# Mixture-of-experts stage on one core: expert outputs added into the output rows tile by tile

## The reference

```python
shared_out = (silu(x @ Wsg.T) * (x @ Wsu.T)) @ Wsd.T          # FS = 704
scores = softmax(x @ Wr.T)                                    # E = 8 experts
topk_scores, topk_idx = top_k(scores, 2)
w_full = sum(one_hot(topk_idx, E) * topk_scores[..., None])
out_e = (silu(x @ Wg[e].T) * (x @ Wu[e].T)) @ Wd[e].T         # F = 352, for every expert e
ffn = einsum('bsed,bse->bsd', out_e, w_full) + shared_out
out = x_before + gb * ffn                                     # gb: one row of 512 per batch
```

## Time and profile before

| what | us |
|---|---|
| median of 3 runs | 1969.69 (1968.26 to 1974.74) |
| profiled execution, span from first to last instruction | 1967.3 |
| busy in the span: TensorE | 1751.4 (89%) |
| VectorE, ScalarE, GpSimd | 1323.2 (67%), 716.7 (36%), 575.9 (29%) |
| GpSimd, the 64 gathers of the combination | 69.2 |

### The profile page before, as it was taken

One profiled execution on the slowest core, in us unless ns is written; L12 is line 12 of the kernel. 1 busy time (PEld: TensorE's weight loads), 2 busy tenths in 40 slices (PEclk: granted clock), 3 DMA queues, 4 the chain that ended last, 5 costly groups with the idle time before them and its releaser, 6 DMA issues.

```text
span 1967.3 us, 29963 instructions
## 1 busy us (share of the span) xinstructions
PE 1751.4 (89%) x9188; PEld 1523.2 (77%) x9188; DVE 1323.2 (67%) x2361; ACT 716.7 (36%) x1146; POOL 575.9 (29%) x691
## 2 busy tenths in 40 slices
PE   4599999997899999997999999999999999999800
PEld 0488888885777777776899999998999999999800
DVE  4899999965898898877432333326666666666566
ACT  2344444443433343333111111115554554554322
POOL 0343333323776676643144410000000000000076
PEclk8799999998998888887999999999999999999955
DMA  8333333327544334322455521105667767667387
GB/s 322 115 122 116 116 116 116 116 84 255 199 145 149 133 134 144 128 89 83 148 181 186 185 92 43 43 22 187 240 231 248 241 230 248 238 232 248 108 260 252
DMA packets 140152, 321.82 MB, mean 164 GB/s; under 512 B 20184, under 2 KB 20184, under 8 KB 134864
## 3 DMA queue, kind: packets, MB, share of 16 engines
q1 hardware_dynamic: 116080, 258.94, 39.4%
q0 software_dynamic: 12800, 41.95, 6.5%
q10 hardware_dynamic: 11232, 20.45, 2.7%
HBM read 213.23 MB, written 108.05 MB: 163 GB/s over the span
## 4 chain that ended last, share of the span: by engine, by line
PE 74%; DVE 14%; POOL 4%; issue 4%; DMA 3%; ACT 1%; SPq 0%; DVEq 0%; POOLq 0%; ACTq 0%
PE bank L424 17%; PE bank L426 17%; PE bank L425 17%; DVE mix L1280 5%; PE bank L1730 5%; PE bank L1728 5%; PE bank L1729 5%; PE bank L435 4%; POOL cb_y L863 3%; PE bank L1722 2%; DVE xh L1265 2%; DVE h_lo L1335 1%; PE bank L1678 1%; DMA stage<-in_w_k 1%; PE bank L1679 1%
## 5 line engine op out<-in xcount | busy, mean ns | idle before, releaser
L424 PE MATMUL bank<-gu_hi,ex_x_hi 128*128 128x352 f32 x1136 | 382.0, 336 | 0.8 <-DVE gu_lo L1362 0.8
L426 PE MATMUL bank<-gu_hi,ex_x_lo 128*128 128x352 f32 x1136 | 369.5, 325 | 0.0
L425 PE MATMUL bank<-gu_lo,ex_x_hi 128*128 128x352 f32 x1136 | 369.2, 325 | 0.0
L863 POOL DMA_INDIRECT cb_y<-expert_out_rows,slots x64 | 69.2, 1081 | 738.9 <-DMA expert_out_rows<-y_rows 719.7
L1478 DVE TENSOR_TENSOR hid<-bank,sg_t 128x352 f32<-128x352 f32 x142 | 74.5, 525 | 307.6 <-ACT sg_t L1015 307.6
L424 PEld LDWEIGHTS bank<-gu_hi,ex_x_hi 128*128 128x128 f32 x1136 | 216.1, 190 | 1.2 <-issue 1.2
L425 PEld LDWEIGHTS bank<-gu_lo,ex_x_hi 128*128 128x128 f32 x1136 | 216.1, 190 | 0.0
L426 PEld LDWEIGHTS bank<-gu_hi,ex_x_lo 128*128 128x128 f32 x1136 | 215.2, 189 | 0.0
L1015 ACT ACTIVATE sg_t<-bank 128x352 f32<-128x352 f32 x142 | 65.8, 464 | 396.6 <-PE bank L426 396.6
L1728 PE MATMUL bank<-dn_hi,hid_hi 128*128 128x512 f32 x426 | 168.0, 394 | 3.1 <-DVE hid_lo L1482 3.1
L1730 PE MATMUL bank<-dn_hi,hid_lo 128*128 128x512 f32 x426 | 168.2, 395 | 0.0
(11 more groups left out here) (214 smaller groups left out, 3999.8 us busy)
## 6 DMA issues: line engine op xcount, KB each, us to landing
raw<-in_ex_gu SPq DMA_DIRECT2D x39, 1408.0 KB, 6.6
expert_in_rows<-zero_rows SPq DMA_DIRECT2D x32, 624.0 KB
raw<-in_ex_dn SPq DMA_DIRECT2D x39, 512.0 KB, 7.5
ex_x<-expert_in_rows SPq DMA_DIRECT2D x78, 256.0 KB, 2.7
expert_out_rows<-y_rows ACTq DMA_DIRECT2D x78, 256.0 KB, 2.0
h_rows<-h_t SPq DMA_DIRECT2D x64, 256.0 KB, 2.6
x_t<-in_x SPq DMA_DIRECT2D x32, 256.0 KB, 2.8
timemix_rows<-o_t SPq DMA_DIRECT2D x32, 256.0 KB, 2.0
```

The costliest lines, as they stand in the source:

```text
L424: pe.matmul(acc, act_hi[i], w_hi[i], start=(i == 0), stop=False)
L425: pe.matmul(acc, act_hi[i], w_lo[i], start=False, stop=False)
L426: last = pe.matmul(acc, act_lo[i], w_hi[i], start=False, stop=(i == chunks - 1))
L863: pool.indirect_dma_start(rows[:, pair % 2, a, :], None, ys_d, bass.IndirectOffsetOnAxis(ap=slots[:, k, n:n + 1], axis=0)).then_inc(arrive ...
```

## The change

Expert rows no longer go through DRAM tables of token rows, and there is no combination stage. A table of 9984 slots with four int32 each (token, target, batch, weight) is made instead: it is first written with an empty entry (token 0, target N, batch 0, weight 0) for every slot, and GpSimd scatters 64 columns of entries of 16 bytes into it where it scattered token rows. SyncE reads the table back into SBUF near the end of the shared stage, one entry of 16 bytes per piece. Rows are gathered straight from `h3_rows` by token. The shared stage keeps `base` in two buffers only and stores each tile to `out`. The zero stores and the row loads of GpSimd go.

In a routed tile j the product of each unit, now in two PSUM banks by turns, is multiplied on VectorE by the slot's weight and by a gathered row of the batch's gate (`gated_unit`), in place of the copy. GpSimd gathers the current `out` rows of the tile's 256 slots (`gather_now`), VectorE adds (`added`, one instruction of 128x1024), and GpSimd scatters the sum back to `out` (`scatter_new`); slots that are padding have a target out of bounds and are skipped. Since two tiles can hold the same token, `gather_now(j)` waits until the scatter of tile j-1 has landed. ScalarE's stores and SyncE's loads of expert rows go.

```diff
-    xs_d = scratch("expert_in_rows", [NJ * R, D])
-    ys_d = scratch("expert_out_rows", [NJ * R, D])
+    gate_d = scratch("gate_of_batch", [B, D])
+    table_d = scratch("slot_table", [NJ * R, 4], I32)
...
@@ SyncE, shared step t
-                    load_residual(t.back(-2))
+                if t.back(1).real():
+                    store_base(t.back(1))
+                if t.back(-1).real():
+                    load_residual(t.back(-1))
...
+                if t.pair is None and t.n == NT - 2:
+                    sp.wait_ge(table_out, 16 * 2 * NT)
+                    sp.dma_start(table[:], table_d.rearrange("(u p) c -> p u c", p=P)).then_inc(table_in, 16)
...
@@ SyncE, routed step t
-                if t.back(-1).real():
-                    load_rows(t.back(-1))
                 if t.real() and t.back(-2).real():
                     load_expert(t.back(-2))
...
@@ GpSimd
             for n in range(NT):
-                if n >= 2:
-                    pool.wait_ge(sc_out[n % 2], 32 * (n // 2))
-                pool.dma_start(sc_t[n % 2], h3_d[n * P:(n + 1) * P, :]).then_inc(sc_in[n % 2], 16)
-                if n >= 1:
-                    scatter(pool, n - 1)
-            scatter(pool, NT - 1)
...
+                for k in range(2):
+                    pool.indirect_dma_start(table_d, bass.IndirectOffsetOnAxis(ap=slots[:, k, n:n + 1], axis=0),
+                                            meta[:, n, k, :], None).then_inc(table_out, 16)
...
+            def gather_x(u):
+                half = u % 2
+                if u >= 2:
+                    pool.wait_ge(*rx_pe.done(u - 2, "turned"))
+                else:
+                    pool.wait_ge(*shx_pe.done(NT - 2 + half, "turned"))
+                pool.indirect_dma_start(ex_x[:, half, :], None, h3_d, index(u, TOKEN)).then_inc(ex_in[half], 16)
+
+            def gather_gate(u):
+                half = u % 2
+                if u >= 2:
+                    pool.wait_ge(*ru_vec.done(u - 2, "gated"))
+                pool.indirect_dma_start(gate_rows[:, half, :], None, gate_d, index(u, BATCH)).then_inc(gate_in[half], 16)
+
+            def gather_now(j):
+                if j >= 1:
+                    pool.wait_ge(new_out, 32 * j)
+                    pool.wait_ge(*sum_vec.done(j - 1, "added"))
+                for half in range(2):
+                    pool.indirect_dma_start(now_rows[:, half, :], None, out_d,
+                                            index(2 * j + half, TOKEN)).then_inc(now_in, 16)
+
+            def scatter_new(j):
+                pool.wait_ge(*sum_vec.done(j, "added"))
+                for half in range(2):
+                    pool.indirect_dma_start(out_d, index(2 * j + half, TARGET), new_rows[:, half, :], None,
+                                            bounds_check=N - 1, oob_is_err=False).then_inc(new_out, 16)
...
+            for j in range(NJ):
+                if 2 * j + 3 < NU:
+                    gather_x(2 * j + 3)
+                gather_gate(2 * j + 1)
+                if 2 * j + 4 < NU:
+                    gather_x(2 * j + 4)
+                if 2 * j + 2 < NU:
+                    gather_gate(2 * j + 2)
+                if j >= 1:
+                    scatter_new(j - 1)
+                gather_now(j)
+            scatter_new(NJ - 1)
+            pool.wait_ge(new_out, 32 * NJ)
...
@@ VectorE
-            def y_of_unit(u, t):
-                if t.back(1).real():
-                    dve.wait_ge(ys_out[u.half], 16 * t.n)
+            def gated_unit(u, t):
+                dve.wait_ge(gate_in[u.half], 16 * t.n + 16)
                 dve.wait_ge(*ru_pe.done(u.n, "down"))
-                dve.tensor_copy(y_rows[:, u.half, :], PS_Y[:]).then_inc(ru_vec.sem_of["y"], 1)
+                dve.scalar_tensor_tensor(add_rows[:, t.p, u.half, :], PS_YR[u.half][:],
+                                         weight_of[:, bass.ds(u.n, 1), WEIGHT:WEIGHT + 1].rearrange("p a b -> p (a b)"),
+                                         gate_rows[:, u.half, :], ALU.mult, ALU.mult).then_inc(ru_vec.sem_of["gated"], 1)
+
+            def added(t):
+                if t.back(1).real():
+                    dve.wait_ge(new_out, 32 * t.n)
+                dve.wait_ge(now_in, 32 * t.n + 32)
+                dve.wait_ge(*ru_vec.done(t.unit(1).n, "gated"))
+                dve.tensor_tensor(new_rows[:], add_rows[:, t.p], now_rows[:], ALU.add).then_inc(sum_vec.sem, 1)
...
                     if before.real():
-                        y_of_unit(before.unit(1 - half), before)
...
+                        gated_unit(before.unit(1 - half), before)
+                    if half and t.back(1).real():
+                        added(t.back(1))
...
@@ TensorE, routed step t
-                        if half == 0 or before.back(1).real():
-                            pe.wait_ge(*ru_vec.done(u.back(1).n, "y"))
-                        else:
+                        if before.back(1).real():
+                            pe.wait_ge(*ru_vec.done(u.back(2).n, "gated"))
+                        elif half:
                             pe.wait_ge(*base_vec.done(NT - 1, "gated"))
```

More of the change, by code:

```diff
@@ L34 @@
 NJ = (2 * N + E * (R - 1)) // R
-ZERO_ROWS = NJ * R // NT
-ZERO_REPEAT = 3
-assert ZERO_ROWS * NT == NJ * R and ZERO_ROWS % ZERO_REPEAT == 0
+NU = NJ * R // P
+TOKEN, TARGET, BATCH, WEIGHT = range(4)
 LN_1E8 = 18.420680743952367
@@ L280, in build @@
             ones = sb("ones", [P, P], at=at)
-        base = sb("base", [P, NT, D])
-        y_rows = sb("y_rows", [P, 2, D])
-        sc_t = [y_rows[:, i, :] for i in range(2)]
+        after_mixing = sb("after_mixing", [P, NT + 2, D])
         gated_t = sb("gated_t", [P, D])
@@ L286, in build @@
         hid_lo = sb("hid_lo", [P, FK, P], F32R)
-        w1 = sb("w1", [P, NT, 1])
-        w2 = sb("w2", [P, NT, 1])
+        w1, w2 = (meta[:, :, k, WEIGHT:WEIGHT + 1].bitcast(F32) for k in range(2))
+        weight_of = table[:].bitcast(F32)
         slots = sb("slots", [P, 2, NT], I32)
@@ L406, in build @@
         ru_act = steps("ru_act", "silu", "hid_hi")
-        ru_vec = Apart(sem, "ru_vec", "hid", "hid_lo", "y")
+        ru_vec = Apart(sem, "ru_vec", "hid", "hid_lo", "gated")
+        sum_vec = steps("sum_vec", "added")
         rw_hi_act = steps("rw_hi_act", "gu_hi", "dn_hi")
         rw_lo_vec = steps("rw_lo_vec", "gu_lo", "dn_lo")
-        cb_act = steps("cb_act", "first")
-        cb_vec = steps("cb_vec", "both", "gated", "out")
         ORDER = W1 + W2
@@ L724, in _ @@
             sweep(sp, NJ, 2, 0, routed_step)
-            def store_out(t):
-                row_of = sp.snap(t.n * 2 * P) if t.pair is not None else t.n * 2 * P
-                sp.wait_ge(*cb_vec.done(t.n, "out"))
-                sp.dma_start(out_d[bass.ds(row_of, 2 * P), :].rearrange("(a p) d -> p a d", p=P),
-                             cb_out[:, t.p]).then_inc(final_out[t.p], 16)
-            sweep(sp, NT // 2, *in_turn((store_out, 0)))
-            for p in range(2):
-                sp.wait_ge(final_out[p], 16 * (NT // 4))
-            sp.wait_ge(zero_out, 16 * NT)
         @block.gpsimd
@@ L841, in _ @@
                                pattern=[[1, P]], channel_multiplier=-1).then_inc(ex_const, 1)
+            for column in range(4):
+                pool.memset(empty[:, :, column], N if column == TARGET else 0).then_inc(meta_ready, 1)
+            for column in (TOKEN, TARGET):
+                pool.iota(meta[:, :, :, column], [[P, NT], [0, 2]], base=0, channel_multiplier=1).then_inc(meta_ready, 1)
+            pool.iota(meta[:, :, :, BATCH], [[1, NT // TPB], [0, TPB], [0, 2]], base=0,
+                      channel_multiplier=0).then_inc(meta_ready, 1)
@@ new lines, in _ @@
+            pool.wait_ge(table_in, 16)
+            pool.wait_ge(gate_out, 16)
+            gather_x(0)
+            gather_x(1)
+            gather_gate(0)
+            gather_x(2)
+            for p in range(2):
+                pool.wait_ge(base_out[p], 16 * (NT // 2))
+            for j in range(NJ):
[9 more added lines that the diff above has]
+                gather_now(j)
@@ L1058, in _ @@
             sweep(act, NT, 1, 1, shared_step)
-            def store_y(t, half):
-                u = t.unit(half)
-                row_of = act.snap(u.n * P) if t.pair is not None else u.n * P
-                act.wait_ge(*ru_vec.done(u.n, "y"))
-                act.dma_start(ys_d[bass.ds(row_of, P), :], y_rows[:, half, :]).then_inc(ys_out[half], 16)
             def routed_step(t):
@@ L1491, in base_of @@
                                   ALU.mult).then_inc(base_vec.sem, 1)
[L1492 removed]
+                rows = base[:, t.p, :]
                 dve.wait_ge(sr_in[t.p], 16 * t.half + 16)
```

139 lines of the change are left out of this document (45 added, 94 removed).

## The result

The changed kernel takes 2153.89 us (median of 4 runs, 2152.76 to 2160.54) against 1968.97 us (4 runs, 1967.5 to 1974.74): ratio 1.0936, 95% interval 1.0910 to 1.0962. The profiled execution has a span of 2151.0 us against 1967.3. The forecast was slower, and slower it is; but the forecast was 1984, and the range ended at 2040.

A forecast was written before the change was run, and what follows sets the result against it. Bound by 39 routed tiles at TensorE's pace, then 102 us of combination. Span 1967.3 - 88.6 (tail) + 102 (loop) + 3 (table read-back) - 2 (shared stage) = 1981.7; median 1984 us, range 1915 to 2040.

The forecast's parts named there:

- The tail: From S_38, the last routed tile's opening transposes, to the end: 31.3 us instead of 119.9, saving 88.6.
- The loop over two steps: Routed stage: sum, scatter, landing, gather_now, gather_x and its landing take 30.9 us, plus 1.6 for the clock; step 16.25.
- 36 periods of 2.84: Routed stage: the slowed steps, S(2) to S(38), each 2.84 us longer than before, 102 us in all.
- (a): Routed loop: the expert load does not hold the scatter, landing 2.8 us, step 13.85, total 1898 us; chance 0.15.
- "nothing": Shared stage: 64 table scatters replace 64 token scatters and 32 loads, covered by the shared tiles, costing no time.
- The -2 for the stall at 982: Shared stage: TensorE's 2.56 us wait for rows behind two expert loads shrinks with less GpSimd traffic; -2 us (0 to -4).
- The read-back of the table: Before the first routed tile: reading 9984 pieces of 16 bytes delays the first gather_x; +3 us, bounds 0 and 22.
- (b): Routed loop: the load holds the scatter but the clock stays whole; step 15.45, total 1955 us; chance 0.19.
- (c): Routed loop: gather_now stretched beside VectorE's gu_lo, gather_x 1.4 us later, 25 us more, total 2009; chance 0.17.
- (d): Routed loop: DMA saturates, landings 5.1 us, burst 1.5 longer, step 1.2 more, total 2027 us; chance 0.09.
- 19.5 GB/s an engine: DMA rate of software-queue gathers and scatters, used to put eight 262 KB transfers at 6.7 us of a step.
- break-even, 15.9: Routed step in us at which the forecast of slower parts from faster; the forecast step was 16.25.

The follow-up runs named there:

- c2: The changed kernel run again unedited on another occasion, where the shared-stage stall was absent: 2095.25 us, span 2093.4.
- c3: The changed kernel run again unedited as control on an occasion with the shared-stage stall: 2158.37 us, span 2156.6.
- e10: Changed kernel with gather of out rows, VectorE sum and plain scatter replaced by one scatter that adds into out in DRAM: span 1987.9 us.
- e11: Changed kernel with the scatter adding in DRAM and each gather of x issued once its buffer is free: 1959.73 us, 0.9954 of before.
- e12: The kernel of e11 with each pair of table scatters held back until the pair before has landed: 1881.80 us, 0.9565 of before.
- e7: Changed kernel with the routed loop's expert loads replaced by three small writes, first two experts' weights serving all tiles: span 2019.3 us.
- e3: Changed kernel with the gather of x for unit 2j+5 issued ahead of the wait for the scatter's landing: span 2017.9 us.
- e4: Changed kernel with SyncE's load of the next expert held until the scatter of the tile before has landed: span 2022.0 us.
- e1: Changed kernel with each pair of table scatters held back until the pair before has landed: span 2087.3 us.
- e1b: The paced table scatters of e1 in the changed kernel again, on the occasion of c2: span 2086.1 us.

## Why the prediction was wrong

**The tail: right but for 8 us.** The sum of the last tile ended 26.4 us after S_38 (27.1 predicted), the last scatter was issued at 28.6 (28.5 predicted) and its issue ended at 2141.27. No further DMA traffic shows behind 2143, yet the span goes on to 2151.0. From the end of GpSimd's last issue to the end of the span it is 9.7 us here as in c2 and c3, and 4.9 to 5.0 in e10, e11 and e12; before, the last store lay within about 1 us of the end. The term was read to the landing and not to the end of the span, and what fills the rest stays open.

**The loop over two steps: right in kind, mis-sized by 5.6 us for two steps.** The failed terms are the landing of gather_x, put at 4.3 us where 7.2 were measured, and the stretched issues of GpSimd, which the sum had at their undisturbed length. Counted from the opening at 1930.10, against the prediction's own steps:

| | predicted | measured |
|---|---|---|
| gate's gather | 15.0 | 17.3 |
| second scatter | 17.7 | 20.6 |
| landed | 23.7 | 27.3 |
| gather_now | 23.8, 25.2 | 27.6, 28.8 |
| gather_x | 26.6 | 30.9 |
| its landing | 30.9 | 38.1 |

1.6 of the 7.2 were foreseen as the clock's (0.89 predicted, 0.88 measured over 1500 to 1800). Of the other 5.6, 2.9 are the landing of gather_x: "landed after 4.3 (3.4 to 5.1)" was taken from the combination of before, where no expert load runs. The prediction had argued that a row moved beside the load waits for it, and then applied this to the scatter alone. SyncE's next load is tied to the step as the scatter is, and falls on gather_x. The rest is GpSimd's: the gate's gather took 1.69 beside the sum on VectorE and stands in front of the scatters, which come 1.3 late beyond the clock's 1.6; the second gather_now took 1.74 instead of 0.97 beside `dn_lo` (0.7). The last 0.7 are the scatter's landing, 6.7 for 6.0.

36 periods of 2.84 were 102 us; the stage grew by 198.

**What was missing in the sum: GpSimd's own cycle.** Eight issues, their pauses and the one wait they stand behind were never added up. e7 shows it: 15.3 us in the mean without loads. So even rival (a), the scatter free of the burst, would hardly have given 13.85 a step.

**The shared stage: "nothing" was wrong.** "The 64 table scatters ... with the shared tiles covering them: nothing" cost 66 us where the stall shows. Their DMA work was small (share 0.07); what was not seen is that the token scatters of before waited for landings between pairs, and these don't (e11 against e12). The -2 for the stall at 982 did not come either: TensorE waited 5.2 and 5.6 us for that load in e3 and e4, against 2.56, and 2.4 in e1, where the scatters are paced. The read-back of the table, +3 (0 to 22), cost nothing: S_0 of c2 is 1333.8 against 1334.1.

**The rivals.** (a) is refuted: 6.2 us beside the load, 2.8 without (e4). The rule of "DMA: Bandwidth & Descriptors", "Queues, rings and completion order", in the Trainium skill, would, as the prediction reads it, have made it the likely one; what was measured beside the load agrees with the trace of before, not with that reading. How the engines shared their time no run shows. (b) is refuted: the clock fell to 0.88, and was 1.00 again when the gaps went (e11). (c) is shown as a mechanism, up to 3.8 us for one issue (first profile, 1938.10), and was no rival but a part of the loop. The row that it was drawn from had the rule already: the gather of 1.78 us in the earlier trace rows ends 0.82 after VectorE's instruction (a product, which the prediction calls a sum), just as here; the prediction took its length for a bound. (d), engines that are full, is refuted by e11, at 0.91 of the DMA engines; its signs came all the same, a later landing and a longer load: the last part of the weights landed 10.7 us after issue in c2, against 8.2 before. The prediction's 19.5 GB/s an engine is 19.3 by the earlier trace rows, which changes nothing in its sums.

What the range left out is not one of them but their sum: two late landings, stretched issues and the low clock lie in one chain and add up. The bounds had been drawn for each alone. Slower was forecast at a step 0.35 us above break-even, 15.9; the measured step, 18.7, is 2.8 above it for terms that the sum did not have, so that the direction came out speaks little for the sum.

**Open.** What differs between the occasions with and without the stall; what the engines wait for in it. The place (the first pass of ScalarE's loop) speaks for the fetch of instructions. The Trainium skill, "Runtime: NRT & Kernel Launch", "Instruction fetch mechanics", says that a taken branch out of the loaded window makes the engine fetch by DMA before it goes on; the stall could be that. The packets of q8 do not show it. In the ten traces without the stall (before among them) the packet lies between 975 and 985; in six of the seven with the stall at 1043 to 1055, in the first profile (1049) 2 us behind ScalarE's restart at 1046.98; but in e11, with a stall of 64.6 us to 1042.82, it came at 989:

```profile
1042.82 0.46 ACT L1025 ACTIVATE sg_t<-bank 128x352 f32<-128x352 f32 x1 [64.63 <-remote]
```

```profile
q8 instruction: 1, 0.02, 1.1%
```

(e11; the second line is from 985 to 990.) So a late packet there is not needed for the stall, and which fetch held which engine, if one did, is not shown. Pacing was not tried alone in the changed kernel while the stall showed.

## What to carry to other kernels

Where one engine issues all the indirect DMAs of a loop, first add up its own cycle, issues, pauses and waits, as one does for TensorE; then look for a gather that stands behind a wait it doesn't need. A landing time belongs to what else is moving at that moment: for every transfer in the chain ask whether a large load is tied to the same step. And where a loop of scatters loses the waits it had, count the waits as part of the change: pacing cost nothing under other work (c2, e1b) and took 78 us off e11.

## What had not been expected of the hardware

- A 256 KB gather or scatter on the software queue took 6 to 7 us beside a 2.1 MB load of weights, 2.8 to 3.5 without it, whichever of them met the load (c2, e4).
- A GpSimd issue of 0.95 us that fell within a VectorE instruction with two SBUF inputs ended 0.8 to 0.9 after it, and so took up to 3.8. A scatter that adds in DRAM took 1.6 (median 1.63 of 78 in e12), a plain one 1.0; the adding one landed in 5.0 us beside the loads (e10, median from 1500 to 1800).
- 64 scatters of 2 KB each, back to back, went with 62 us in which the three compute engines nearly stood still, on some occasions and not on others, always for all unpaced kernels of an occasion, and ending 6 to 9 us after the last of the scatters was issued.
- 16 DMA engines ran at 0.91 busy over 400 us with TensorE 98% busy beside them (e11).
